# A network of two graph layers and two feed-forward layers: the routed experts' weights move from SyncE's queue to indirect gathers on GpSimd

## The reference

```python
router_probs = softmax(flat @ router_w + router_b)          # 8 experts
topk_probs, topk_idx = top_k(router_probs, 2)
shared_out = gelu(flat @ sw1 + sb1) @ sw2 + sb2
h1 = gelu(einsum('td,edh->teh', flat, rw1) + rb1)           # rw1: 8 x 1024 x 256
expert_out = einsum('teh,ehd->ted', h1, rw2) + rb2          # rw2: 8 x 256 x 1024
mixed = einsum('ted,te->td', expert_out, weights)           # weights: 0 but for the chosen two
out = x + shared_out + mixed
```

## Time and profile before

| | us |
|---|---|
| median of 3 runs | 3461.34 |
| lowest and highest | 3457.65, 3465.45 |
| the profiled execution, its own time | 3464.66 |
| its span | 3462.7 |

### The profile page before, as it was taken

How to read it: one execution, slowest core, us unless ns; L and a number is a source line. 1 busy time by engine, 2 the same in 40 slices (tenths; PEclk the granted TensorE clock), 3 DMA queues, 4 the chain that set the end, 5 groups by cost and what they waited for, 6 DMA issues and landing times. The chain is left out here.

```text
span 3462.7 us, 49907 instructions
## 1 busy us (share of the span) xinstructions
PE 2829.3 (82%) x13634; PEld 2215.3 (64%) x13634; DVE 2412.9 (70%) x5211; ACT 1440.8 (42%) x2803; POOL 1771.3 (51%) x1604
## 2 busy tenths in 40 slices
PE   0997102999998899989899899999996897299996
PEld 0786101444444678967677688888885887288885
DVE  6232703999998665267777899999997554567774
ACT  1221001333333544333333577777774332155554
POOL 3777875667665474277776344444442111023332
PEclk9999556999999997699999899999998887599999
DMA  3333524999998012011111588877775242389997
GB/s 102 82 91 97 161 80 161 352 351 340 350 350 284 1 67 104 14 20 27 21 27 20 187 260 260 261 261 260 261 260 196 99 145 83 133 251 286 279 283 179
DMA packets 222560, 609.87 MB, mean 176 GB/s; under 512 B 45851, under 2 KB 84114, under 8 KB 222302
## 3 DMA queue, kind: packets, MB, share of 16 engines
q0 software_dynamic: 139008, 429.63, 39.6%
q1 hardware_dynamic: 83422, 178.63, 15.1%
HBM read 522.69 MB, written 85.11 MB: 176 GB/s over the span
## 5 line engine op out<-in xcount | busy, mean ns | idle before, releaser
L656 POOL DMA_INDIRECT g_rows<-z_rows,edge_src x704 | 695.8, 988 | 603.9 <-PE g_totals L1430 317.0
L711 PE MATMUL g_sums<-g_rows,g_share 128*128 128x512 f32 x704 | 332.5, 595 | 183.7 <-DMA g_rows<-z_rows,edge_src 183.7
L497 POOL DMA_INDIRECT edge_list<-payload,row_i x320 | 400.1, 1250 | 147.5 <-issue 94.4
L1093 POOL DMA_INDIRECT shared<-el_rows,edge_src x352 | 335.1, 952 | 172.0 <-issue 107.0
L697 ACT ACTIVATE g_scaled_hi<-g_rows,edge_weight_sorted 128x1024 fp32r<-128x1024 f32 x176 | 202.7, 1152 | 512.8 <-DMA g_rows<-z_rows,edge_src 503.7
L1423 PE MATMUL g_sums<-g_rows,g_share 128*128 128x256 f32 x1408 | 350.0, 392 | 0.0
L711 PEld LDWEIGHTS g_sums<-g_rows,g_share 128*128 128x128 f32 x704 | 133.3, 189 | 284.4 <-issue 269.1
L1375 ACT ACTIVATE g_scaled_hi<-g_rows,g_factor 128x256 fp32r<-128x256 f32 x704 | 300.0, 496 | 4.0 <-DMA g_rows<-z_rows,edge_src 1.8
L1499 DVE SCALAR_TENSOR_TENSOR g_scaled_lo<-g_rows,g_factor,g_scaled_hi 128x256 fp32r<-128x256 f32 x704 | 293.4, 479 | 1.3 <-ACT g_scaled_hi L1375 1.1
L1423 PEld LDWEIGHTS g_sums<-g_rows,g_share 128*128 128x128 f32 x1408 | 256.2, 192 | 28.1
L1278 DVE TENSOR_REDUCE t_largest<-t_masked 128x4 f32<-128x512 f32 x352 | 231.6, 685 | 50.2 <-PE t_masked L1160 43.8
(11 more groups left out here) (372 smaller groups left out, 7585.4 us busy)
## 6 DMA issues: line engine op xcount, KB each, us to landing
e_raw<-in_L_ffn_rw_dram SPq DMA_DIRECT2D x56, 1024.0 KB, 7.0
g_rows<-z_rows,edge_src POOLq DMA_INDIRECT x704, 5.5
z_rows<-z_zout SPq DMA_DIRECT2D x20, 512.0 KB, 3.0
x_rows<-x_all SPq DMA_DIRECT2D x20, 512.0 KB
z_rows<-t_zout SPq DMA_DIRECT2D x20, 512.0 KB, 2.7
s_x<-x_rows SPq DMA_DIRECT2D x10, 1024.0 KB, 8.7
xn_rows<-s_rows SPq DMA_DIRECT2D x10, 1024.0 KB, 4.1
z_x<-in_x_dram SPq DMA_DIRECT2D x19, 512.0 KB, 4.2
```

What stands on the lines that cost most here:

```text
L497: pool.indirect_dma_start(out=g.lists[k], out_offset=bass.IndirectOffsetOnAxis(ap=row_i[0:EP, c:c + 1], axis=0), in_=payload[0:EP, c, :], ...
L656: pool.indirect_dma_start(out=r.rows[:, slot, :], out_offset=None, in_=table, in_offset=bass.IndirectOffsetOnAxis(ap=g.src[:, i * GT + q:i ...
L711: nc.tensor.matmul(sums[:, k, h, :], share[:, k, :], r.rows[:, k * GT, h * HALF:(h + 1) * HALF], start=True, stop=False)
L1093: pool.indirect_dma_start(out=g.edge_el[:, n, :], out_offset=None, in_=g.el, in_offset=bass.IndirectOffsetOnAxis(ap=g.src[:, n:n + 1], axi ...
```

## The change

The routed weights are first copied in DRAM, in the attention stage, into two tables, `w1_rows` and `w2_rows`, in which the 8 KB that one partition of a weight buffer takes are one row (row expert x 128 + partition). Sixteen transfers of 1 MB on SyncE's queue do that, behind the chunks of W1 and ahead of the store of the scores.

Routing computes a row index for each partition and group, `weight_row`. Where a group's expert is that of the group two back, 1024 is added, which puts the index outside the table; the gather is issued with a bound and leaves such rows out.

In the expert stage `raw1` and `raw2` get two buffers each. GpSimd fetches the weights of a group with two indirect gathers at the head of the step before the group's own, ahead of that step's row gathers (those of group 0 before all). SyncE only loads the bias tables, `all_bias2` now ahead of everything but the two small ones and with a semaphore of its own, for which VectorE waits before the first output; ScalarE waits for the small tables alone.

```diff
             for c in range(KD):
                 at_least(sp, w_low, c - 1)
                 sp.dma_start(zout[:, c % 2, :].rearrange("p (h f) -> p h f", h=HEADS), w_rows[c]).then_inc(w_in[c % 2], 16)
+            for e in range(EXPERTS):
+                sp.dma_start(g.w1_rows[e * P:(e + 1) * P, :].rearrange("p (c f) -> p c f", c=KD),
+                             g.rw1[e].rearrange("(c p) f -> p c f", p=P)).then_inc(relaid, 16)
+                sp.dma_start(g.w2_rows[e * P:(e + 1) * P, :].rearrange("p (m n) -> p m n", m=2),
+                             g.rw2[e].rearrange("(m p) n -> p m n", p=P)).then_inc(relaid, 16)
             sp.wait_ge(scores_kept, NT)
...
                 sp.wait_ge(stored[k], 16 * (NT // 2))
+            sp.wait_ge(relaid, 16 * 2 * EXPERTS)
...
+            q.iota(partition[:], pattern=[[0, 1]], base=0, channel_multiplier=1, **small)
+            q.memset(repeats[:], 0.0)
             q.memset(ones[:], 1.0)
             q.memset(none[:], 0.0)
...
             st.done(v.tensor_scalar(g.expert[:], group_count[:], float(EXPERTS - 1), None, ALU.min))
+            st.link(v.tensor_scalar(group_count[:], group_count[:], float(EXPERTS - 1), None, ALU.min))
+            st.done(v.tensor_tensor(repeats[:, 2:PG], group_count[:, 2:PG], group_count[:, 0:PG - 2], ALU.is_equal))
+            st.link(v.tensor_scalar(row_of[:], group_count[:], float(P), partition[:, 0:1], ALU.mult, ALU.add))
+            st.done(v.scalar_tensor_tensor(out=g.weight_row[:], in0=repeats[:], scalar=float(EXPERTS * P), in1=row_of[:],
+                                           op0=ALU.mult, op1=ALU.add))
 
             dve.wait_ge(pairs_sorted, 1)
             st.link(v.tensor_copy(held[:], sorted_pairs[:, 0:PT]))
...
-        raw1, raw2 = sb("raw1", [P, KD * EH]), sb("raw2", [P, 2 * D])
+        raw1, raw2 = sb("raw1", [P, 2, KD * EH]), sb("raw2", [P, 2, 2 * D])
...
+        raw1_in, raw2_in = ([a.sem(f"e_raw{n}_in{k}") for k in range(2)] for n in (1, 2))
...
-            for i in range(PG):
-                e = sp.value_load(g.expert[0:1, i:i + 1], min_val=0, max_val=EXPERTS - 1)
-                at_least(sp, m.raw1_used, i)
-                sp.dma_start(raw1[:].rearrange("p (c f) -> p c f", c=KD),
-                             g.rw1.rearrange("e (c p) f -> p (e c) f", p=P)[:, bass.ds(e * KD, KD), :]).then_inc(m.raw1_in, 16)
-                at_least(sp, m.raw2_used, i)
-                sp.dma_start(raw2[:].rearrange("p (m n) -> p m n", m=2),
-                             g.rw2.rearrange("e (m p) n -> p (e m) n", p=P)[:, bass.ds(e * 2, 2), :]).then_inc(m.raw2_in, 16)
-                if i == 0:
-                    sp.dma_start(all_bias2[:], g.rb2.rearrange("e d -> (e d)").partition_broadcast(P)).then_inc(m.small_in, 16)
+            sp.dma_start(all_bias2[:], g.rb2.rearrange("e d -> (e d)").partition_broadcast(P)).then_inc(m.bias2_in, 16)
 
         @block.gpsimd
         def _(pool):
+            def weights(i):
+                for raw, table, used, arrived in ((raw1, g.w1_rows, m.raw1_used, raw1_in),
+                                                  (raw2, g.w2_rows, m.raw2_used, raw2_in)):
+                    at_least(pool, used, i - 1)
+                    pool.indirect_dma_start(
+                        out=raw[:, i % 2, :], out_offset=None, in_=table,
+                        in_offset=bass.IndirectOffsetOnAxis(ap=g.weight_row[:, i:i + 1], axis=0),
+                        bounds_check=EXPERTS * P - 1, oob_is_err=False).then_inc(arrived[i % 2], 16)
+
+            weights(0)
+
             def body(item):
                 it = item(0)
                 if it:
                     k = it.i % 2
+                    if it.i + 1 < PG:
+                        weights(it.i + 1)
                     at_least(pool, m.turned_ready, (it.i - 1) * GT)
                     for q in range(GT):
...
-            act.wait_ge(m.small_in, 48)
+            act.wait_ge(m.small_in, 32)
...
-                    act.wait_ge(m.raw1_in, (it.i + 1) * 16)
+                    act.wait_ge(raw1_in[k], (it.i // 2 + 1) * 16)
                     at_least(act, m.hidden_ready, it.i - 1)
-                    s.copy(w1_hi[:, k].rearrange("p c f -> p (c f)"), raw1[:]).then_inc(m.w1_high, 1)
-                    act.wait_ge(m.raw2_in, (it.i + 1) * 16)
+                    s.copy(w1_hi[:, k].rearrange("p c f -> p (c f)"), raw1[:, k, :]).then_inc(m.w1_high, 1)
+                    act.wait_ge(raw2_in[k], (it.i // 2 + 1) * 16)
                     at_least(act, m.y_ready, (it.i - 1) * GT)
-                    s.copy(w2_hi[:, k].rearrange("p m n -> p (m n)"), raw2[:]).then_inc(m.w2_high, 1)
+                    s.copy(w2_hi[:, k].rearrange("p m n -> p (m n)"), raw2[:, k, :]).then_inc(m.w2_high, 1)
...
-            dve.wait_ge(m.small_in, 48)
...
                             e = dve.value_load(g.expert[0:1, it.i:it.i + 1], min_val=0, max_val=EXPERTS - 1)
                             shift = all_bias2[:, bass.ds(e * D, D)]
+                        if n == 0:
+                            dve.wait_ge(m.bias2_in, 16)
                         dve.wait_ge(m.y_ready, n + 1)
                         at_least(dve, y_added, (it.i - 1) * GT * 16)
...
-                    dve.wait_ge(m.raw1_in, (it.i + 1) * 16)
+                    dve.wait_ge(raw1_in[k], (it.i // 2 + 1) * 16)
                     dve.wait_ge(m.w1_high, it.i + 1)
-                    split_vector(v, w1_lo[:, k].rearrange("p c f -> p (c f)"), raw1[:],
+                    split_vector(v, w1_lo[:, k].rearrange("p c f -> p (c f)"), raw1[:, k, :],
                                  w1_hi[:, k].rearrange("p c f -> p (c f)"), m.raw1_used)
...
+        w1_rows=scratch("w1_rows", [EXPERTS * P, KD * EH]), w2_rows=scratch("w2_rows", [EXPERTS * P, 2 * D]),
```

More of the change, by code:

```diff
@@ L1054, in stage_attention @@
         el_in = [sem(f"el_in{b}") for b in range(NB)]
-        stored = [sem(f"stored{k}") for k in range(2)]
+        stored, relaid = [sem(f"stored{k}") for k in range(2)], sem("relaid")
         (w_high, w_low, std_ready, rstd_ready, xn_ready, turned_ready, hi_ready, lo_ready, scores_ready,
@@ L1805, in stage_route @@
         of_group = sb("of_group", [P, PG, EXPERTS])
-        group_count = sb("group_count", [P, PG])
+        group_count, row_of = sb("group_count", [P, PG]), sb("row_of", [P, PG])
+        repeats, partition = sb("repeats", [P, PG]), sb("partition", [P, 1])
         at_row, at_col = sb("at_row", [P, ALL, P], F32R), sb("at_col", [P, ALL, 3, PT], F32R)
@@ L1992, in stage_experts @@
         hidden = a.psum("e_hidden", [P, HALF])
-        names = ("small_in raw1_in raw2_in raw1_used raw2_used w1_high w2_high v_done turned_ready "
-                 "hi_ready lo_ready hidden_ready act_ready split_ready y_ready y_kept y_scaled bias1_ready").split()
+        names = ("small_in raw1_used raw2_used w1_high w2_high v_done turned_ready "
+                 "hi_ready lo_ready hidden_ready act_ready split_ready y_ready y_kept y_scaled bias1_ready bias2_in").split()
         m = Named(**{n: a.sem(f"e_{n}") for n in names})
@@ L2146, in body @@
                     k = it.i % 2
-                    dve.wait_ge(m.raw1_in, (it.i + 1) * 16)
+                    dve.wait_ge(raw1_in[k], (it.i // 2 + 1) * 16)
                     dve.wait_ge(m.w1_high, it.i + 1)
-                    split_vector(v, w1_lo[:, k].rearrange("p c f -> p (c f)"), raw1[:],
+                    split_vector(v, w1_lo[:, k].rearrange("p c f -> p (c f)"), raw1[:, k, :],
                                  w1_hi[:, k].rearrange("p c f -> p (c f)"), m.raw1_used)
-                    dve.wait_ge(m.raw2_in, (it.i + 1) * 16)
+                    dve.wait_ge(raw2_in[k], (it.i // 2 + 1) * 16)
                     dve.wait_ge(m.w2_high, it.i + 1)
-                    split_vector(v, w2_lo[:, k].rearrange("p m n -> p (m n)"), raw2[:],
+                    split_vector(v, w2_lo[:, k].rearrange("p m n -> p (m n)"), raw2[:, k, :],
                                  w2_hi[:, k].rearrange("p m n -> p (m n)"), m.raw2_used)
@@ L2204, in build @@
         g.expert = a.sb("group_expert", [P, PG], I32)
+        g.weight_row = a.sb("weight_row", [P, PG], I32)
         g.sorted_token = a.sb("sorted_token", [P, PT], I32)
```

## The result

| | before | after |
|---|---|---|
| median of 7 runs, us | 3466.54 | 3481.3 |
| lowest and highest | 3457.65, 3471.49 | 3471.8, 3484.61 |
| profiled execution, its own time | 3464.66 | 3481.3 |
| its span | 3462.7 | 3479.5 |

The ratio after to before is 1.0036, 95% interval [1.0025, 1.0047]: on 3466.54 us that is a loss of 12.5 us (8.7 to 16.3). The two medians are 14.8 us apart, the spans of the two profiled executions 16.8. The prediction was 3475, slower.

The account below looks back on a forecast made before the run. TensorE's work plus a 1.2 us handover was taken to set the expert step, not DMA traffic. Stalls +15.5, opening −1.3 and routing +0.2 gave +14.4 us: 3475 on the three-run median 3461.3, range 3456 to 3494.

Parts of the forecast that it names:

- The sum: Whole kernel: stalls +15.5, opening −1.3, routing +0.2, together +14.4 us on the execution of 3464.66 us.
- What bounds the kernel: Expert stage: TensorE's work plus 1.2 us handover sets the step; less DMA traffic buys nothing; rows have 0.7 us spare.
- Which groups stall: Expert stage: 11 of 28 groups fetch; of consecutive fetches first and third stall, the second does not; five stalls.
- What a stall costs: Fetching steps: weights ahead of rows in the ring, 3.1 us each, 15.5 in all (10.5 to 19); signs 2 to 4.
- GpSimd's two extra gathers: Steady steps without fetch: 1.30 us each (bounds 0 and 1.9), no cost, covered by DMA time the weights leave.
- Opening: Start of expert stage: first cast at 3018, hidden(0) at 3024.8, gain 1.3 us (bounds 4 gained, 2 lost).
- Copy: Attention stage: sixteen 1 MB DRAM transfers fit in 67.6 us, taken as hidden; 16 us late at the lower rate.
- (a): Attention stage: the copy is late, 3491 us, or 3502 if it runs at 179 GB/s; chance 0.20.
- Routing: Routing stage: two more GpSimd instructions cost +0.2 us; four on VectorE, some 0.8 us, lie in its 6.12 us wait.
- (b): Expert stage: no stalls, rows overtake or the fetch is quicker; only small terms left, 3460, no change; chance 0.17.
- (d): Expert stage: the skip doesn't skip, every group fetches, 12 × 3.1 = 37 us, 3498; chance 0.06.
- (c): Opening: ring served ahead of the bias, cast at 3009, hidden(0) at 3016, −10; without stalls 3450; chance 0.12.

Follow-up runs that it names:

- rows first, all fetch: Changed kernel with each step's row gathers ahead of the weight gathers and all 28 groups fetching their weights; ratio 0.9976 to the kernel before.
- All fetch: Changed kernel with the index never moved outside the table, so all 28 groups fetch their weights; ratio 1.0114 to the kernel before.
- no refetch: Changed kernel with weights of groups 2 to 27 never fetched, their gathers issued but all skipped; ratio 0.9980 to the kernel before.
- empty gathers: Kernel before plus the DRAM copies and two all-skipped gathers per step ahead of the row gathers; ratio 0.9998 to the kernel before.
- bias alone: Kernel before with only a separate semaphore for the 4 MB bias table, so ScalarE waits for the small tables alone; ratio 0.9976.
- Rows first: Changed kernel with each step's two row gathers issued ahead of the next group's two weight gathers; ratio 0.9967 to the kernel before.
- rows first, bias late: Changed kernel with row gathers ahead of weight gathers in every step, the first too, and the bias table issued after group 0's second weight; ratio 0.9958.
- copy alone: Kernel before with only the sixteen DRAM copies of the weights and the wait for them added; ratio 1.0003 to the kernel before.
- half refetch: Changed kernel with the second weight of groups 2 to 27 never fetched; ratio 1.0003 to the kernel before.

## Why the prediction was right, and where it was off

**The total: right in part by luck.** The sum was +14.4 us; the spans differ by 16.8. The stalls cost 7.4 us more than in the sum, the opening (first cast and first step) gained 1.0 more, 2.7 came off at the end of the span, and the part ahead of the stage, +0.2 in the sum, shows −1.3. The errors nearly cancel. That 3475 lies below 3481.3 has another cause too: it was reckoned from a median of three runs, 3461.34, and the median of seven is 3466.54. What held was the mechanism, below.

**What bounds the kernel: shown.** With less weight traffic the steps stayed at 14.88 us, and with all of it too (rows first, all fetch). One reading was too clean: TensorE did have two steady waits for rows before, of 0.8 and 0.2 us, so the spare was sometimes used up already.

**Which groups stall: shown.** The five waits are where the sum put them: the rows of groups 3, 11, 13, 19 and 21, each behind the weights of the group after it. All fetch bore out the two-step pace roughly.

**What a stall costs: the step that was mis-sized.** The sum had 5 × 3.1 = 15.5 (bounds 10.5 to 19); measured were 22.9, outside the bounds. Three errors met in it.

First, the length of a wait. These are the second scatters ahead of the five waits, from issue to landing:

```profile
3048.80 7.01 DMA out_dram<-e_y_out,sorted_token
3172.74 7.72 DMA out_dram<-e_y_out,sorted_token
3206.54 7.05 DMA out_dram<-e_y_out,sorted_token
3299.76 7.48 DMA out_dram<-e_y_out,sorted_token
3334.85 7.57 DMA out_dram<-e_y_out,sorted_token
```

They land after 7.4 us in the mean, where 6.90 was taken. From the landing to TensorE's transposes (3064.40, 3187.71, 3221.20, 3314.86, 3349.67) pass 8.6, 7.3, 7.6, 7.6 and 7.3 us. The mean of 7.7 us is 342 GB/s for 2.62 MB: the slow end of the bracket (348), not its middle. So the wait was 4.3 us in the mean, not 3.1; the signs had 2 to 4, and four of the five were longer. The Trainium skill, "DMA: Bandwidth & Descriptors", section "Anatomy of one DMA — SWDGE (gpsimd) path", has a fixed 2.0 us beside the rate. By the rate alone, as the prediction used it, the wait would have been 2.3 us, and the trace does not bear that out. With the 2.0 us counted once the transfer is 8.0 us, an estimate by that page, and the five measured ones lie on both sides of it.

Second and third, I priced a wait at its own length. It costs less by the handover wait that it swallows, and more by the clock. The table of waits shows the first: e_y's waits fell from 35.8 us (no refetch) to 29.3, so 21.3 − 6.5 = 14.8 us of pure delay. The second is in the windows behind the five waits: (0.28 + 0.25 + 0.28 + 0.46 + 0.40) × 6 = 10.0 us of full clock lost. Together 24.8 for the 22.9 measured. That the sum's 15.5 is near the pure delay is chance, since waits too short by 5.8 us and a handover left out by 6.5 cancel; the fall of the clock was in no term.

**GpSimd's two extra gathers: right value, wrong reason.** Start to start they take 1.3 us, as taken. But "the cover is the DMA time that the weights leave" failed: with the weights' full traffic they cost nothing either (empty gathers). There the rows landed only 1.0 us later for being issued 2.7 us later; the backlog of the ring behind the scatters would explain it. The 0.7 us of spare was also too small a figure, since up to some 1.2 us of wait are swallowed by the handover.

**Opening.** Right in its form, gain 3.0 us at hidden(0) for 1.3 predicted, inside the bounds. The first transposes came 24.2 us after the first gather, on the scale of the kernel before at 3014.4, within 3013 to 3018.5; tile 1 was turned 2.4 us behind the cast (2.5 predicted), hidden(0) 6.7 behind it (6.8). Waiting for the bias was worth 12 us at hidden(0), as bias alone showed, and 9 of them were lost again. Rows first won back 5.1 of these, by two weight gathers fewer ahead of the first rows; rows first, bias late won a further 5.4.

**Copy.** Hidden, by its own run. 16.8 MB went in the 58 us from 1372, at 289 GB/s or more of payload. So the 179 GB/s of rival (a) are refuted by that row. The Trainium skill's "HBM Reference", section "Specifications (TRN2)", gives the share for two cores streaming at once and says that a core alone gets more; this program runs on one core.

**Routing.** +0.2 us can't be seen; VectorE's wait for TensorE fell from 6.12 to 5.45 us, near the 0.8 us that its four instructions were to take from it.

**Missed.** 2.7 us less at the end of the span, behind the last scatter. It is there in each kernel whose SyncE no longer loads the weights (36.6 to 37.4 us from the last first-tile cast, against 39.4 to 39.7 in the four others). No run tells what it is, and the sum had no term for it.

**Rivals.** (a) falls by copy alone, (b) by the waits, (d) by the 135 GB/s of the seven steps without a fetch, where all fetch has 246; all fetch also shows what (d) would have cost, 52 us more in the stage than before. (c) falls by the first cast of rows, 26.2 us after the first gather where it had some 19; what it forecast at hidden(0) came only with the rows ahead of the weights and the bias late.

## What to carry to other kernels

In one queue that serves transfers in order, sort by when each is needed: what is needed in this step goes ahead of what is needed in the next, however cheap its issue is. Moving a load to another queue is first a change of what stands in front of what, and only then a change of bytes. Before pricing a wait, look which other wait it will swallow, and whether the granted clock falls behind it.

## What the runs showed of the hardware

- A wait of TensorE for rows of 1.3 to 2.1 us left the clock at 1.00 (half refetch: the transposes behind it 1.09 us); each of the five waits of 3.9 to 4.9 us in the changed kernel was followed by the 0.50 level. In between it went either way: in all fetch a wait of 3.60 us was followed by transposes of 1.09 us and one of 2.23 us by 1.97. So the length of the wait alone does not decide.

```profile
3822.13 1.09 PE L2076 MATMUL e_turned<-ident,e_rows 128*128 128x128 f32 x8 [3.60 <-DMA e_rows<-xn_rows,sorted_token]
...
3837.68 1.97 PE L2076 MATMUL e_turned<-ident,e_rows 128*128 128x128 f32 x8 [2.23 <-DMA e_rows<-xn_rows,sorted_token]
```

- An indirect gather of which every index is out of bounds costs GpSimd as much as one that fetches: 1.05 and 1.01 us, 1.3 start to start. The skip saves bytes only.
- Row gathers issued 2.7 us later behind the scatters landed only 1.0 us later (empty gathers, medians).
- A copy from DRAM to DRAM ran at 289 GB/s of payload or more beside a busy TensorE (58.00 of 58.00 us), and copy alone took as long as the kernel before: 1.0003, with an interval of 0.001 to either side.
